# Where GpSimd copies the indices of a convolution's gathers: behind the fourth gather, or behind the wait for landed rows

## The reference

```python
y0 = x0 @ W_l1_0 * inv * a                    # per node, 32 channels
y1 = einsum('nuc,uv->nvc', x1, W_l1_1) * ...   # per node, 3 x 32 channels
h = silu(edge_scalars @ W_fc1 / sqrt(10)); w = h @ W_fc2 / sqrt(100)
x0e, x1e = y0[edge_src], y1[edge_src]          # one row of 128 floats per edge
edge_feat = concat(w00*x0e*sh0, w11*dot(x1e, sh1), w01*x0e*sh1, w10*x1e*sh0)
sums = segment_sum(edge_feat, edge_dst, num_segments=n)
```

## Time and profile before

| | us |
|---|---|
| median of 3 runs | 9076.38 |
| lowest and highest of them | 9073.87, 9081.07 |
| time of the profiled execution | 9026.2 |
| its span | 9024.4 |

### The profile page before, as it was taken

The page is one execution under the profiler, slowest core; times in us unless marked ns, Lnnn a source line. Parts: engine busy times, 40 slices in busy tenths (PEclk is TensorE's granted clock), DMA queues, the critical chain, the costliest instruction groups (busy, mean ns, idle before and its releaser), DMA issues. The chain is left out here.

```text
span 9024.4 us, 195785 instructions
## 1 busy us (share of the span) xinstructions
PE 7554.3 (84%) x51013; PEld 5691.8 (63%) x51014; DVE 6072.0 (67%) x12579; ACT 5237.7 (58%) x9302; POOL 3483.8 (39%) x4082
## 2 busy tenths in 40 slices
PE   5999999888869998899989978777777877777774
PEld 3666666587769996666666655555656665566664
DVE  7888998899964446555555555556666666666666
ACT  3666666688857775444444433336666666566663
POOL 0000000000000001666666666664666666666665
PEclk8999999999989998899999887889999899889997
DMA  3333333466646662222222211113555555555554
GB/s 112 137 137 134 137 138 139 146 234 220 226 127 183 183 183 77 62 63 62 62 61 62 59 47 46 46 46 114 168 171 168 167 165 172 165 163 167 171 172 129
DMA packets 511185, 1177.42 MB, mean 130 GB/s; under 512 B 98171, under 2 KB 171308, under 8 KB 491685
## 3 DMA queue, kind: packets, MB, share of 16 engines
q1 hardware_dynamic: 381834, 858.67, 29.2%
q0 software_dynamic: 129280, 317.93, 12.6%
HBM read 899.64 MB, written 276.57 MB: 130 GB/s over the span
## 5 line engine op out<-in xcount | busy, mean ns | idle before, releaser
L2263 POOL DMA_INDIRECT att_kv_rows<-kv_dram,att_stage x1616 | 1657.1, 1025 | 1021.4 <-issue 679.0
L2002 POOL DMA_INDIRECT conv_rows<-y_dram,conv_stage x1616 | 1576.9, 976 | 876.3 <-issue 616.7
L1967 ACT ACTIVATE conv_hid<-conv_hid_ps 100x512 f32<-100x512 f32 x408 | 243.3, 596 | 1145.0 <-DMA y_dram<-mean_nodes_both 785.9
L695 PE MATMUL conv_part<-conv_msgs,conv_hot 128*128 128x256 f32 x3232 | 900.0, 428 | 5.0 <-issue 4.6
L842 PE MATMUL att_mlp<-mlp_feats,mlp_w 64*128 64x512 f32 x1568 | 534.6, 738 | 409.6 <-ACT mlp_hid L862 348.1
L851 PE MATMUL att_mlp<-mlp_w,mlp_hid 128*128 128x128 f32 x6272 | 770.9, 283 | 42.4 <-issue 24.4
L851 PEld LDWEIGHTS att_mlp<-mlp_w,mlp_hid 128*128 128x128 f32 x6272 | 748.4, 199 | 61.6 <-issue 39.6
L695 PEld LDWEIGHTS conv_part<-conv_msgs,conv_hot 128*128 128x128 f32 x3232 | 677.2, 221 | 105.5 <-issue 10.6
L235 PE MATMUL count_ps<-count_cols,count_rows 128*128 128x392 bf16 x3920 | 730.1, 332 | 8.5 <-DVE count_cols L201 8.5
L862 ACT ACTIVATE mlp_hid<-att_mlp,mlp_b 128x512 f32<-128x512 f32 x784 | 498.4, 684 | 379.7 <-PE att_mlp L842 256.2
L2035 PEld LDWEIGHTS conv_w_ps<-conv_w,conv_hid 100*128 100x128 f32 x3248 | 458.8, 217 | 396.4 <-issue 365.7
(11 more groups left out here) (278 smaller groups left out, 16280.7 us busy)
## 6 DMA issues: line engine op xcount, KB each, us to landing
c_dram<-count_counts SPq DMA_DIRECT2D x392, 392.0 KB, 2.4
mean_counts<-c_dram SPq DMA_DIRECT2D x343, 448.0 KB, 3.4
w_dram<-mlp_w SPq DMA_DIRECT2D x404, 256.0 KB
att_w_rows<-w_dram SPq DMA_DIRECT2D x404, 256.0 KB
soft_counts<-c_dram SPq DMA_DIRECT2D x98, 1024.0 KB, 4.8
mlp_feats<-in_feats SPq DMA_DIRECT2D x405, 192.0 KB
soft_counts<-c_dram SPq DMA_DIRECT2D x49, 1088.0 KB, 5.0
att_lanes<-lo_dram SPq DMA_DIRECT2D x404, 128.0 KB
```

The lines of the kernel that those rows point to most:

```text
L695: ins = nc.tensor.matmul(part, c.hot[:, s, t, :], rows[:, t, :], start=half == 0 and t == 0, stop=half == 1 and t == T - 1)
L2002: pool.indirect_dma_start(rows[:, s, t, :], None, y_dram, bass.IndirectOffsetOnAxis(ap=stage[:, s, t:t + 1], axis=0)).then_inc((gathered[s ...
L2263: pool.indirect_dma_start(kv_rows[:, s, t, :], None, kv_dram, bass.IndirectOffsetOnAxis(ap=stage[:, s, t:t + 1], axis=0)).then_inc((gather ...
```

## The change

In every round of the convolution, `take` for the round after next, with the two waits for the gathers that used its slot, stands ahead of the round's own four gathers instead of behind them. Since the round before ends with the wait for its first three landed gathers, the copy comes behind that wait. What is copied, into which slot, for which round, and all semaphores and counts stay as they are. Attention keeps its order, and both keep eight rounds in the loop.

```diff
                 def body(i, first, last=False):
                     for s in range(S):
                         g = S * i + s
-                        pool.wait_ge(staged, g + 1)
-                        pool.wait_ge(rows_used, S * i + s + 1)
-                        pool.sem_inc(turn, 1)
-                        for t in range(T):
-                            pool.indirect_dma_start(
-                                rows[:, s, t, :], None, y_dram,
-                                bass.IndirectOffsetOnAxis(ap=stage[:, s, t:t + 1], axis=0)).then_inc((gathered[s] if t < T - 1 else gathered_last[s]), 16)
                         if s < 2 or not last:
                             if s >= 2:
                                 pool.wait_ge(gathered[s - 2], 16 * (T - 1) * (i + 1))
                                 pool.wait_ge(gathered_last[s - 2], 16 * (i + 1))
...
                             take((s + 2) % S, g + 2)
+
+                        pool.wait_ge(staged, g + 1)
+                        pool.wait_ge(rows_used, S * i + s + 1)
+                        pool.sem_inc(turn, 1)
+                        for t in range(T):
+                            pool.indirect_dma_start(
+                                rows[:, s, t, :], None, y_dram,
+                                bass.IndirectOffsetOnAxis(ap=stage[:, s, t:t + 1], axis=0)).then_inc((gathered[s] if t < T - 1 else gathered_last[s]), 16)
 
                         pool.wait_ge(gathered[s], 16 * (T - 1) * (i + 1))
```

## The result

| | before | after |
|---|---|---|
| median, us | 9075.39 (4 runs) | 9151.64 (4 runs) |
| lowest and highest | 9073.87, 9081.07 | 9145.39, 9159.94 |
| profiled execution, its span | 9026.2, 9024.4 | 9159.94, 9158.1 |

The ratio after to before is 1.0083, 95% interval 1.0066 to 1.0101. The sign was forecast, the size was not: 9151.64 us lies above the range of 9076 to 9140 us. Every profiled execution from here on is one of the timed ones of its kernel. The profile of before is not: 9026.2 us lies outside 9073.87 to 9081.07 us, and the record does not say that it was taken together with them.

A forecast was written before the change was run, and what follows sets the result against it. PE was taken to pace the convolution with MLP units, POOL's chain many rounds without. Growth of 40 and 60 us less slack of 19 and 55 left 21 + 5 = 26 us; 9026.2 + 26 + 50.2 gave 9102 us, range 9076 to 9140.

The forecast's parts named there:

- POOL's chain and the shadow of the landing: Convolution: the third gather's landing starts POOL's next round, hiding the copy; POOL's chain is 95% of a second-stretch round.
- The price, 0.25 us a round: Convolution: register step and copy behind the landing lengthen POOL's chain by 0.25 us a round, 100 us over 401 rounds.
- only the steps: Lower bound of the price: the copy fits in the gather's 0.8 us start, only sequencer instructions count, 0.07 us.
- register step and copy in series: Price on POOL's path as 0.055 us register instruction plus 0.192 us median copy, together 0.247 us.
- Hidden after all: Rival: the copy runs within the gather's start, 0.07 us a round within the slack; 9076 us; chance 0.22.
- dear start: Rival: POOL starts twice behind each landing, 0.5 us a round, together 126 us, 9202 us; chance 0.10.
- the change does nothing: Rival: the sequencer might run the copy ahead of the wait; 9076 us; chance 0.02.
- Faster: Rival: the moved copy no longer holds up DVE's products, 0.04 us a round, 16 us less, 9060 us; chance 0.04.
- The slack, 19 and 55 us: POOL's waits for a free slot absorb growth: 19 us in the second convolution stretch, 55 us in the first.
- The busy nine tenths of PE: First part of the convolution: PE busy nine tenths, so PE sets the pace there and POOL is mostly ahead.
- The 50.2 us between profile and median: The median of the runs lies 50.2 us above the profiled execution; added to 9052 us to give 9102 us.
- The second and first stretch, 21 and 5 us: Convolution without MLP units lengthens by 21 us, with MLP units by 5 us, after slack; sum 26 us.

The follow-up runs named there:

- copy_at_3: Kernel before with the convolution's copy and its two waits put between a round's third and fourth gather; 9059.59 us against 9062.96 us for before.
- three_steps: Kernel before, copy in its old place, three extra semaphore increments on POOL behind the wait ending each convolution round; 9178.36 us against 9062.96 us.
- jobs 2 and 5: Chip runs of both unchanged kernels beside variants: after 8986.21 against before 8932.07 us in the first, 9015.14 against 9064.4 us in the second.
- quiet jobs: Jobs whose kernels show only 1 register or branch instruction over 0.3 us in the convolution; the kernel before takes 9063 to 9075 us there.
- c_before: Kernel before, unchanged, profiled again beside the unchanged kernel after; 8934.69 us, convolution 2470.1 us.
- c_before3: Kernel before, unchanged, profiled again in a later job; 9053.61 us, convolution 2575.0 us.
- before_pad: Kernel before with eight unused semaphore increments on POOL behind the convolution's last round, shifting later code; 8938.06 us against 8932.07 us.
- job 1: The first pair of kernels: before 9075.39 us, after 9151.64 us.
- copy_at_3_b: copy_at_3 repeated in job 6; 9055.17 us against 9063.83 us for before.
- stalled jobs: Jobs with many register or branch instructions over 0.3 us in the convolution, 108 in c_before and 161 in c_before3; before takes 8932 to 9064 us.
- early_conv: Kernel before with each convolution round ending in a wait for its first two landed gathers, not three; 9226.69 us against 9054.16 us.
- the early kernels: Four kernels whose convolution rounds wait for two landed gathers instead of three, some with further changes; 9224.5 to 9716.3 us.
- job 6: Repetition of three_steps (9176.16 us) and copy_at_3 (9055.17 us) beside the kernel before (9063.83 us).
- job 4: Runs with the shorter wait for landed gathers, and the unchanged kernel after (9011.62 us), beside the kernel before (9054.16 us).

## Why the prediction was wrong

**POOL's chain and the shadow of the landing: right.** copy_at_3 (copy still ahead of the fourth gather's end: nothing lost) and three_steps (no copy moved: 115 us lost) bear it out from both sides. The estimate of 2.15 us from the Trainium skill (DMA: Bandwidth & Descriptors, "Anatomy of one DMA — SWDGE (gpsimd) path"), against which this reading was weighed, does not agree with the trace of after either: from the third gather's start at 5251.58 the wait would have ended at 5253.73, and its copy's register step is seen at 5254.1.

**The price, 0.25 us a round: right in kind, a third too high.** The gap grew by 0.17 us between the first two profiles and by 0.16 to 0.18 us in jobs 2 and 5; between the quiet jobs it is 0.20 us longer in after than in copy_at_3. The loss of 76 us over 404 rounds is 0.19 us. I added a copy's duration of 0.192 us to its register step of 0.055 us. Two steps at the 0.095 us of three_steps would be 0.19 us too; how the price divides between the register step and the copy no run tells, but a second copy costs 0.07 to 0.12 us, less than it runs. Between my "only the steps" (0.07 us) and "register step and copy in series" (0.247 us) the measured price lies two thirds of the way up. The rivals fall with it. "Hidden after all" priced the steps at their recorded 0.07 us, where they cost more; "dear start" would have made the gap pass 2.8 us; "the change does nothing" has the copy ahead of the wait, and it starts behind it. "Faster" by freeing DVE is not seen: its product on the rows takes 547/559/630 ns after and 545/559/635 before. The sentence on the copy's mean duration adds wrongly: with 0.28 us its sum is 38 us and not 33.

**The slack, 19 and 55 us: this is the step that failed.** I read 161.5 us of POOL's waits for a free slot as room that the kernel has, and let it absorb 74 of 100 us. That room was a property of the profiled execution: 99 us there, 26 us in c_before, 130 us in c_before3, and nothing in copy_at_3, the quiet kernel that has the time of before. (41 of the 97 waits were not at a round's start; counted rightly, that profile would have absorbed even more.)

No profile of the kernel before in a quiet job was kept, but the time of its convolution can be worked out: about 2450 us. This follows three times over from a profile's convolution and that execution's distance to the median of before: 2531.4 - 84.6 = 2447 us (after), 2445.2 + 11.3 = 2457 us (copy_at_3), 2574.1 - 120.6 = 2454 us (three_steps), if all the rest of the kernel takes what it takes in before.

The other profiles bear it out: the convolution less POOL's room (the waits at a round's start beyond 0.9 us each) is 2450 us in the profile of before, 2444 in c_before, 2454 in before_pad, 2445 in c_before3 and 2445 in copy_at_3. So POOL's own chain is nearly the same in all of them, and what the wait for a free slot held was time that other engines had added. In the kernel after POOL has no such waits in any job, and its convolution is 2450 us and the growth of the gap (65 to 81 us) in all four profiles: 2515 to 2531 us. The profile shown has 2549 us, some 100 us that the timed runs of job 1 do not have.

With no slack the working of the prediction gives 404 x 0.25 = 101 us with its own price, and 404 x 0.17 to 0.20 = 69 to 81 us with the growth of the gap. Measured: 76 us. The busy nine tenths of PE misled in the same way. After the change PE was busy 1400 of 1544 us with 6871 instructions, before it 1403 us with 6678, and yet after it DVE waited for POOL's rows in 398 of 404 rounds.

**The 50.2 us between profile and median, carried over as a constant: wrong.** It was no constant around the same stages. Attention was 152 us longer in job 1 (by the profile of after) and the convolution of before about 2549 - 2450 = 99 us shorter, together 53 us more. Three timed runs lay within 7.2 us of each other, and the profiled execution 47.7 us below the lowest of them. That was the warning: an execution so far outside its companions is made of other stage times, and its slack isn't theirs.

**The second and first stretch, 21 and 5 us: wrong with the slack.** In the quiet jobs the first stretch goes from about 6.08 us a round (copy_at_3_b 6.07, copy_at_3 6.10) to 6.28, the second from 5.94 to 6.21. Over 241 and 160 rounds that is 48 and 43 us.

**Attention as long as before: right,** by the pairs of jobs 2 (2760 and 2762.5 us) and 5 (2797 both), and not by the first two profiles.

**What stays open.** In stalled jobs the change is worth +54, -43 and -49 us. The two gains need the kernel before to lose, in its other engines, time that the kernel after does not lose; why an earlier gather would do that is open. And early_conv, whose POOL is quicker, costs 173 us. The order of each engine's program is fixed, so I take it that an earlier gather does harm through something shared; no run shows what. What makes a register instruction take 0.7 us in one job and 0.05 us in another, with the same program and data, no row here tells. Nor did any run show the early kernels in a quiet job. They may be a gain there; that they lose is shown for stalled jobs alone. Loading of code was a candidate. The Trainium skill (Runtime: NRT & Kernel Launch, "Instruction fetch mechanics") has a taken branch wait for a transfer when its target lies outside the two pages that are loaded. By it a loop that does not fit into two pages would add transfers at every turn. The instruction queues of after (quiet) and of c_before3 (stalled), packets, MB and share, do not differ:

```profile
q8 instruction: 30, 0.49, 0.0%
q14 instruction: 41, 0.34, 0.0%
```

Both pages have these same two lines, 71 packets in the whole span, where POOL's loop alone takes some 50 turns in the convolution: the trace shows no transfer of code for each turn, and no difference between the kinds. No version tried here was shown to beat the kernel before in both kinds of job; copy_at_3 equals it in the quiet one.

## What to carry to other kernels

Behind a wait for a transfer that sets the pace, count every step of the sequencer, here 0.08 to 0.1 us each and more than the 0.043 us that the profile records for one, and not the whole execution of what they start; 0.19 us in 404 rounds are 76 us. Take an engine's slack from one profile only if that execution's time lies among the timed ones, and count only waits longer than the pause that is there anyway; if the time lies outside, work out the stage's floor from the pacing engine's own cycle (start to start 5.87 us in the earlier trace rows, 2371 us over 404 rounds, to which the longer gaps at the loop's turns add; copy_at_3 took 2445 us) and price the change without the slack as well. Compare stages between two profiles only within one job: here the untouched stage differed by up to 152 us between profiles of different jobs, and by 2.5 us between before and after within job 2.

## What the runs showed of the hardware

- From the end of POOL's last sequencer step to the start of the indirect gather it is 0.73 us where the engine is idle (median in 16 of 20 profiles). A 0.184 us copy dispatched just ahead of that step runs inside it.
- A semaphore step of POOL's sequencer behind a wait costs 0.09 to 0.095 us a round (three_steps, 115 us and 112 us for three in 404 rounds); the register step is recorded with 0.055 us and the semaphore step with 0.043 us.
- The copy itself is steadier behind the landing: 183/184/307 ns min/median/max over 404, against 186/192/619 in the shadow of the fourth gather. No run shows a gain from that.
- The same program on the same data ran in two ways, by the job: register steps of at most 65 ns, or up to 727 ns and over; attention's wait at slot 0 of 6.0 us or about 4 us. The totals of the kernel before lay 10 us apart (9063.83 us in job 6 and 9054.16 us in job 4, on a chip of one number), so the median alone does not tell them apart, though the spread of the runs did (7 to 17 us against 38 to 55 us). The change had opposite signs: +76 us in a quiet job, +54, -43 and -49 us in stalled ones.
